# A GNN, mixer and FFN block on one core: the input norm written out with three buffers of x, and the first gathers and products placed inside the batch statistics

## The reference

```python
xn = _layernorm(x)
x = x + gnn(xn, edge_weight, W1, b1, W2, b2, eps, src, dst) + mix(xn[None])[0]
x = x + ffn(_layernorm(x)[None])[0]

def gnn(x, edge_val, ...):
    agg = jax.ops.segment_sum(edge_val[:, None] * x[edge_src], edge_dst, num_segments=N)
    h = jax.nn.relu(((1.0 + eps) * x + agg) @ W1.T + b1)
    return h @ W2.T + b2

def mix(x, ...):
    h = logmap0(proj(x, c), c)                    # a factor for each node
    h = conv1d(h, w_qkv, pad=2)                   # for a sequence of one: a 256 to 768 product
    h = relu(batchnorm(h, bn_gamma, bn_beta))     # mean and variance over all nodes
    ...                                           # linear attention in groups of 32, w_res, expmap0
```

## Time and profile before

| | us |
|---|---|
| median of 3 runs (2632.32 to 2636.76) | 2632.83 |
| the profiled execution: its time | 2637.63 |
| its span in the profile | 2636.0 |
| PE busy | 2489.5 (94%) |
| DVE busy | 1806.4 (69%) |
| ACT busy | 1464.7 (56%) |
| POOL busy (issuing gathers for the most part) | 1753.3 (67%) |

### The profile page before, as it was taken

One profiled execution on the slowest core, in us unless ns is written; L12 is line 12 of the kernel. 1 busy time (PEld: TensorE's weight loads), 2 busy tenths in 40 slices (PEclk: granted clock), 3 DMA queues, 4 the chain that ended last, 5 costly groups with the idle time before them and its releaser, 6 DMA issues.

```text
span 2636.0 us, 42907 instructions
## 1 busy us (share of the span) xinstructions
PE 2489.5 (94%) x12654; PEld 2172.5 (82%) x12654; DVE 1806.4 (69%) x5986; ACT 1464.7 (56%) x3513; POOL 1753.3 (67%) x1858
## 2 busy tenths in 40 slices
PE   5688899999999999999999999999999999999997
PEld 4466688888888888888888888888788888888886
DVE  5754676767767677776776867667676776777657
ACT  4453555655556565565655556556565655656531
POOL 0006777777777777777777777777777777777600
PEclk9798999999999999999999999999999999999998
DMA  7433444344444444434344444443434444343338
GB/s 228 153 115 88 119 118 127 114 121 124 120 125 115 120 124 120 125 116 128 115 121 123 117 126 114 121 123 115 126 115 126 118 121 121 111 129 114 108 116 278
DMA packets 195537, 333.37 MB, mean 126 GB/s; under 512 B 47839, under 2 KB 138013, under 8 KB 195209
## 3 DMA queue, kind: packets, MB, share of 16 engines
q0 software_dynamic: 85216, 233.60, 31.1%
q1 hardware_dynamic: 105018, 92.42, 10.9%
q10 hardware_dynamic: 5072, 4.57, 0.6%
HBM read 291.99 MB, written 38.46 MB: 125 GB/s over the span
## 4 chain that ended last, share of the span: by engine, by line
PE 76%; DVE 9%; ACT 6%; DMA 6%; issue 2%; ACTq 1%; POOL 1%; SPq 0%; DVEq 0%; POOLq 0%
PE bank L1168 23%; PE qkv L1263 13%; PE bank L1275 12%; PE bank L1182 9%; PE bank L1212 6%; PE qkv L1192 4%; DMA work<-in_x 4%; PE qkv L1191 2%; PE bank L1228 2%; PE bank L1237 2%; PE bank L1202 2%; DVE rings L975 2%; DMA rings<-xn_dram,window 1%; DVE work L407 1%; ACT work L465 1%
## 5 line engine op out<-in xcount | busy, mean ns | idle before, releaser
L781 POOL DMA_INDIRECT rings<-xn_dram,window x1764 | 1740.5, 987 | 651.3 <-issue 381.4
L1168 PE MATMUL bank<-rings 128*128 128x256 f32 x3528 | 891.9, 381 | 28.1 <-DMA rings<-xn_dram,window 16.3
L1168 PEld LDWEIGHTS bank<-rings 128*128 128x128 f32 x3528 | 654.6, 190 | 130.2 <-DVE rings L975 32.8
L975 DVE TENSOR_SCALAR rings<-iota,window_dst,window 128x128 f32<-128x128 f32 x1764 | 559.8, 364 | 150.3 <-PE bank L1168 136.2
L1263 PE MATMUL qkv<-work,ffn_weights 128*128 128x256 f32 x1568 | 362.9, 380 | 0.0
L1275 PE MATMUL bank<-ffn_weights,work 128*128 128x256 f32 x1568 | 362.0, 379 | 0.0
L871 ACT ACTIVATE work<-qkv,fb 128x256 f32<-128x256 f32 x392 | 159.6, 472 | 310.5 <-PE qkv L1263 309.9
L1275 PEld LDWEIGHTS bank<-ffn_weights,work 128*128 128x128 f32 x1568 | 297.2, 190 | 40.0
L1263 PEld LDWEIGHTS qkv<-work,ffn_weights 128*128 128x128 f32 x1568 | 293.9, 190 | 37.8
L1182 PE MATMUL bank<-resident,weights 128*128 128x256 f32 x1176 | 279.0, 381 | 0.0
L1182 PEld LDWEIGHTS bank<-resident,weights 128*128 128x128 f32 x1176 | 224.5, 191 | 30.7
(11 more groups left out here) (222 smaller groups left out, 3332.5 us busy)
## 6 DMA issues: line engine op xcount, KB each, us to landing
rings<-xn_dram,window POOLq DMA_INDIRECT x1764, 2.8
xn_dram<-work SPq DMA_DIRECT2D x14, 896.0 KB, 7.7
work<-xn_dram SPq DMA_DIRECT2D x49, 256.0 KB, 3.1
work<-in_x SPq DMA_DIRECT2D x48, 256.0 KB
out<-work SPq DMA_DIRECT2D x48, 256.0 KB
work<-in_x SPq DMA_DIRECT2D x13, 896.0 KB, 5.9
rings<-out SPq DMA_DIRECT2D x6, 896.0 KB, 8.6
out<-rings SPq DMA_DIRECT2D x6, 896.0 KB, 6.8
```

The costliest lines, as they stand in the source:

```text
L781: nc.gpsimd.indirect_dma_start(out=msg[q][:, :], out_offset=None, in_=xn_dram[:, :], in_offset=bass.IndirectOffsetOnAxis(ap=window[t % WIN ...
L975: v.tensor_scalar(sel[k % SEL_RING], iota[:, :], window_dst[b][:, k % SLOTS:k % SLOTS + 1], window[b][:, k % SLOTS, 2:3].bitcast(F32), ALU ...
L1168: te.matmul(agg[h][:, 0:D], sel[k % SEL_RING], msg[q], start=first, stop=last, skip_group_check=True).then_inc(slot_used, 1)
```

## The change

Names of files' lines below are those before (-) and after (+); the rest of the program is the same.

- **Norm.** `x` has three buffers (the third in the ring of `msg`). All 14 groups are written out. DVE's work is split: `stats(g)` and `result(g)`, in the order stats 0, stats 1, result 0, stats 2, result 1, stats 3, and so on. In `result` the logarithm's input is made before the normalised rows are written.
- **ACT** asks for the logarithm ahead of the copies of the group before, and then takes copy and scale by turns. It issues no loads: the 21 loads of the weights are POOL's (`params_pool`), behind the first transfers of the tables.
- **Tables.** `tables_ends` is DVE's first work, `tables_chunks` comes after result 2, `tables_borders` after result 4. The load of `dst` is POOL's first instruction.
- **Start of the main loop.** The dummy product that frees the ring comes before the batch statistics. DVE makes the first 12 one-hots, and PE does the means' products, two thirds of `mix_h1(0)` and the first 12 edge products, inside the statistics. The products of the Gram matrix go to other PSUM banks.

```diff
+        xb = [view(work, 0, G, D), view(work, 1792, G, D), view(rings, 11 * D, G, D)]
+            for g in range(3):
+                load(g)
+            for g in range(NG):
+                sp.wait_ge(xn_ready, g + 1)
+                if g + 3 < NG:
+                    load(g + 3)
+                store(g)
...
+            tables_ends(dve)
+            stats(0)
+            stats(1)
+            for g in range(NG):
+                result(g)
+                if g == NG - 4:
+                    dve.wait_ge(xn_ready, NG - 3)
+                    v.memset(xb[(NG - 1) % 3][:, G - 1], 0.0).then_inc(xlast_clear, 1)
+                if g == 2:
+                    tables_chunks(dve)
+                if g == 4:
+                    tables_borders(dve)
+                if g + 2 < NG:
+                    stats(g + 2)
...
+            rsqrt_table(0)
+            for g in range(NG):
+                if g + 1 < NG:
+                    rsqrt_table(g + 1)
+                log(g)
+                for k in range(G):
+                    if g > 0:
+                        copy(g - 1, k)
+                    scale(g, k)
...
+            early(0, 6)
             dve.wait_ge(gw_done, 1)
...
             ins.then_inc(gw_read, 1)
+            early(6, EARLY_EDGES)
             dve.wait_ge(stat_done, 1)
...
             pe.wait_ge(bounds_landed, 16)
+            pe.wait_ge(h0T_ready, NT)
+            te.matmul(agg[0][:, 0:1], ident[:, :], ident[:, 0:1], start=True, stop=True).then_inc(slot_used, RING)
+            bn_products(pe)
+            mix_h1(0, 0)
+            mix_h1(0, 1)
+            bn_moments(pe)
+            for k in range(EARLY_EDGES):
+                edge(0, k)
             pe.wait_ge(bn_ready, 1)
-            te.matmul(agg[0][:, 0:1], ident[:, :], ident[:, 0:1], start=True, stop=True).then_inc(slot_used, RING)
-            te.matmul(agg[0][:, 0:1], ident[:, :], ident[:, 0:1], start=True, stop=True).then_inc(rem_used, 1)
-            for q in range(3):
-                mix_h1(0, q)
+            te.matmul(agg[1][:, 0:1], ident[:, :], ident[:, 0:1], start=True, stop=True).then_inc(rem_used, 1)
+            mix_h1(0, 2)
```

More of the change, by code:

```diff
@@ L22 @@
 LEAD = 8
+EARLY_EDGES = 12
 WINDOWS = 4
@@ L353, in norm_sync @@
         def norm_sync(sp):
[L354 to L377, removed]
+            def load(g):
+                if g < NG - 1:
+                    sp.dma_start(xb[g % 3], node_rows(x, g * G, G)).then_inc(x_landed[g % 3], 16)
+                else:
+                    sp.dma_start(xb[g % 3][:, 0:G - 1], node_rows(x, g * G, G - 1)).then_inc(x_landed[g % 3], 16)
+                    sp.wait_ge(xlast_clear, 1)
+                    sp.dma_start(xb[g % 3][0:LAST, G - 1], x[(NT - 1) * P:N, :]).then_inc(x_landed[g % 3], 16)
@@ L379, in build, with store, norm_vector, stats @@
+            def store(g):
+                sp.dma_start(node_rows(xn_dram, g * G, G), xnb[g % 2]).then_inc(xn_stored[g % 2], 16)
+            for g in range(3):
[5 more added lines that the diff above has]
+                store(g)
         stats_ready = sem("stats_ready")
-        def norm_vector(dve, stats_turn):
+        def norm_vector(dve):
             v = nc.vector
-            def step(g, h, landed, before):
+            def stats(g):
+                h = g % 2
+                link = Link(dve, stats_link, 1, g)
+                part, mv, var = view(st[h], 0, G, 6), view(st[h], 42, G, 2), norm_cols(h)[0]
+                dve.wait_ge(x_landed[g % 3], 16 * (g // 3 + 1) + (16 if g == NG - 1 else 0))
+                for k in range(G):
+                    ins = v.bn_stats(part[:, k], xb[g % 3][:, k])
+                ins.then_inc(stats_ready, 1)
+                dve.wait_ge(stats_ready, g + 1)
+                for k in range(G - 1):
+                    v.bn_aggr(mv[:, k], part[:, k])
+                link(v.bn_aggr(mv[:, G - 1], part[:, G - 1]))
+                v.tensor_scalar(var[:, 0], mv[:, :, 1], LN_EPS, None, ALU.add)
+                v.tensor_scalar(var[:, 1], mv[:, :, 1], TINY, None, ALU.add).then_inc(var_ready, 1)
+                link.close()
+            def result(g):
+                h = g % 2
@@ L396, in step @@
[L396 to L400, removed]
                 dve.wait_ge(rsqrt_seed, g + 1)
                 newton(v, link, y, var, t)
-                if before is not None:
-                    dve.wait_ge(xn_stored[h], before * 16)
-                    dve.wait_ge(h0_ready, before * (2 * G) + (h - 1) * G)
@@ L1071, in step @@
                     nxt = ahead >= STEP_SLOTS
-                    if not (last and nxt):
+                    if not (last and nxt) and not (i == 0 and ahead < EARLY_EDGES):
                         edge(i + nxt, ahead % STEP_SLOTS)
@@ L1116, in step, with early @@
                     tail.close()
-            dve.wait_ge(bounds_landed, 16)
-            start_tile(0)
-            for k in range(LEAD):
-                edge(0, k)
+            def early(first, n):
+                if first == 0:
+                    dve.wait_ge(bounds_landed, 16)
+                    start_tile(0)
+                for k in range(first, n):
+                    edge(0, k)
+            bn_vector(dve, early)
             for i in range(NS):
```

163 lines of the change are left out of this document (61 added, 102 removed).

## The result

| | before, us | after, us |
|---|---|---|
| median of 4 runs each | 2633.18 (2632.32 to 2636.76) | 2601.06 (2598.36 to 2602.23) |
| the profiled execution: its time | 2637.63 | 2601.07 |
| its span | 2636.0 | 2599.4 |
| start of the Gram products (A) | 188.10 | 166.72 |
| start of step 2 (B) | 307.73 | 267.35 |

The changed kernel is faster: ratio 0.9874, 95% interval 0.9857 to 0.9891. By the medians that is 32.1 us, by the two profiled executions 36.6. The forecast was 49.8 for the profiled pair, and by medians a time of 2583: the measured 2601.06 is 18 above it. A came 21.4 earlier (32 forecast), B 40.4 (49.7 forecast), and behind B some of it went again.

What follows compares the result with a forecast made beforehand. Latency (DVE's waits) bounds the norm, then POOL's gathers set the pace to B. A = 156, B = 258 against 307.7: 49.8 off 2637.63 gives 2587.8, by medians 2583; forecast proper 2575 to 2591, range 2572 to 2604.

Steps and rivals of the forecast that it cites:

- the rivals at 2593 to 2596: Longer norm period 2596 (0.22), steps 0 and 1 bound by their chain 2593 (0.10), POOL's issues blocking DVE 2595 (0.06).
- a longer period of the norm: Norm: slow-landing loads or PE at low clock lengthen each group, to 8.8 us for a load; 2596, chance 0.22.
- Length of a group: Norm: DVE's 10.34 us per group without its three waits becomes 7.80; not below PE's 7.6.
- Loads moved to POOL: Norm: weights' loads run beside x from about 18 us, exposing only group 3's load; cost taken as 0, at most 4.
- The other tables: Norm: tables_chunks and tables_borders block DVE 17.8 us as before, including 4.21 waiting for the gather of borders.
- Start: Start of the norm: dst lands at 9.5 us (bounds 8 and 14), first factor ready at 26.3.
- Last group: End of the norm: last factor at 145.5, plus PE's tiles and low-clock restart, gives A = 156, 32 earlier.
- A to B: First mixer product at A + 31.2, new POOL wait 4.1, B at A + 101.9, so 258.
- B hangs on when the first gather goes, and not on the chain: Steps 0 and 1: 72 gathers at 1.30 us, 93.6 us, set the pace; B comes 97.6 after the first.
- the rival with the chain as the bound: Steps 0 and 1: without edges to fill with, PE waits for ACT and DVE in the mixer; 10 us lost, 2593, chance 0.10.
- An earlier start is kept: Behind B: PE and POOL are close, and the earlier start stays whichever bounds; 49.8 us off the profiled execution.
- The rival on POOL's issues and DVE: Norm: DVE waits while POOL writes descriptors; 21 issues of 0.55 give up to 11.6 us, 2595, chance 0.06.

Runs made afterwards that it cites:

- the experiment: Changed kernel with POOL issuing the 21 weight loads ahead of the tables' transfers: 2992.84 us against before's 3029.73, ratio 0.9887.
- The experiment that asks earlier: Changed kernel with the gather of borders asked for right after the chunks, used after result 4 as before: 2990.71 us, ratio 0.9874 to before.
- the first pair: The original measurement of the kernel before and the changed kernel, chip not on record: medians 2633.18 and 2601.06 us, ratio 0.9874.
- the four chips: Chips of the follow-up runs, where every kernel takes 15 to 16% longer than at first; the kernel before takes 3029.73 to 3052.34 us.
- second chip: Before 3050.42 us; changed kernel 3026.86; changed norm with the ring freed after the batch statistics and no early one-hots, mix_h1 or edges 3024.47.
- first chip: Before 3029.73 us; changed norm with ring freed after the statistics 3004.05; changed kernel with ring freed early, no early edge products 2999.57.
- without the early edges: Changed kernel with no edge product before step 0 and 8 early one-hots for 12, ring still freed early: 2999.57 us, ratio 0.99 to before.
- both waits gone: Changed kernel with weights' loads ahead of the tables' and borders asked for early: 3005.01 us, ratio 0.9853; repeated 3008.05, 0.9869.

## Why the prediction was right in direction, and 13 us too high in gain

The time of 2601.06 lies inside the forecast range of 2572 to 2604, near its far end, and outside the 2575 to 2591 of the forecast proper. What carried the range so far up were the rivals at 2593 to 2596, and the likeliest of them, a longer period of the norm, did not come about. So the range held in part by luck. One sign that the prediction had named for being wrong did appear, once: x's landing ended a wait of DVE. By the prediction's own steps:

- **Length of a group: right, and on the safe side.** 7.80 was taken, DVE takes 7.41. All three waits went as worked out. PE with 7.6 is therefore the bound, not DVE. Its restart "at the low clock", taken as 1, cost 1.6 behind the borders; from 120 to 140 the clock is 1.00.
- **Loads moved to POOL: the step that failed.** "Taken as 0, at most 4"; it is 8.29, and the experiment puts it down to the weights. The prediction counted the queues' time for x alone, at 77%, and set the weights beside it without adding their bytes. In the window from 20 to 40 the DMA engines are at 92%, and x takes 15.8 us to land. The 10 us of `tables_chunks`, which were to let the queues drain, come after the wait and not before it.
- **The other tables: mis-sized.** The 4.21 for the borders were carried over; it was 7.59. The wait before, as a window, and the wait after:

```profile
88.00:94.40 6.40, 0.00 (x0) 0.00 (x0) 2.13 (x4) 0.00 (x0) 2.04 (x2) 0.64 0.07 16
```

```profile
76.00:84.20 8.20, 8.20 (x47) 7.04 (x46) 0.63 (x4) 5.97 (x31) 2.05 (x2) 1.00 0.86 257
```

The gather had the DMA engines to itself (7% busy) and now runs beside x at 86%; a gather of borders takes 6.3 us from issue to landing, and took 2.5. The experiment that asks earlier gains 9.5 at A.
- **Start: mis-sized.** `dst` let DVE go at 11.71, not 9.5; it was inside the bounds of 8 to 14. First factor at 28.06, not 26.3.
- **Last group.** Start 1.8 late, x 8.3, borders 3.4, less 13 x 0.39 = 5.1 for the shorter group, make 8.4; the last factor was 7.5 late (153.03, 145.5 forecast). From there to A it took 13.7, not 10.5, because PE had a backlog as the new bound. Together 10.7: A at 166.72, not 156.
- **A to B: right in the sum (100.6, forecast 101.9), but by other terms, which is luck in part.** The means took 2.73 and the second moments 2.99, not 5.2 each, and with this the first mixer block stood at A + 24.2 and not A + 31.2. The 0.50 of the earlier trace rows did not come back, and the rows put this down to the new order behind A (no kernel here has that order with the old norm, which would show it alone). The kernel before had the full clock at A as well, and lost it behind a stand; a window of its Gram products, its first one-column products, and a window of the changed kernel's means:

```profile
188.10:193.50 5.40, 5.40 (x16) 2.95 (x16) 1.18 (x7) 0.00 (x0) 0.00 (x0) 1.00 0.01 2
```

```profile
195.57 1.02 PE L595 MATMUL bank<-rings,work 128*128 128x1 f32 x4 [2.04 <-DVE work L567]
```

```profile
172.00:174.60 2.60, 2.60 (x26) 2.60 (x24) 2.42 (x7) 0.00 (x0) 1.99 (x3) 1.00 0.40 112
```

  Before, PE stood 2.04 us for DVE between the two, and the clock was 0.50 from 196 on. Now the means and `mix_h1`, which need nothing from DVE, fill that place, and PE does not stand between A and 190. (It is at 0.90 in the second moments and at 0.79 in the twelve edges, 6.85 us for a forecast of 7.2.) The prediction had this order in its list and priced it at the old clock.

  Of the 7 us so gained 4.9 went again in step 0: from its first mixer block to step 1 it took 228.81 - 190.87 = 37.9, for a forecast of 33. There PE stood 7.32 for ACT, did the second mixer block at 0.50 in 3.8 us instead of 2, and stood 1.94 for a one-hot. Step 1 took 267.35 - 228.81 = 38.5, as forecast (38.3).

  POOL waited 0.69 and 1.21 where 0.30 is usual, 1.3 more and not 4.1. And "B hangs on when the first gather goes, and not on the chain" was true of the kernel before and is not of the changed one, in which PE waits for no gather up to B. This is the rival with the chain as the bound (0.10), hidden by the gain in the statistics.
- **"An earlier start is kept": not in full in this pair.** The gap was 40.4 at B, 43.1 at step 3, and 36.6 at the end. Single steps differ by up to three us either way between the two executions. The last step that lies between two starts, as a window of after and of before:

```profile
2421.80:2471.90 50.10, 45.88 (x220) 38.77 (x219) 29.30 (x93) 25.45 (x55) 24.48 (x55) 0.93 0.30 83
```

```profile
2461.80:2508.70 46.90, 42.94 (x220) 36.60 (x219) 29.19 (x93) 25.34 (x55) 26.45 (x56) 1.00 0.33 92
```

The same 220 products took 2.94 more of PE's time, at a granted clock of 0.93 instead of 1.00. That is 2.9 of the 6.5 us lost between step 3 and the end. Why the clock fell there in one and not in the other no run shows; the other 3.6 us are not explained.

**The rival on POOL's issues and DVE** did not come about. The changed kernel's POOL at two of the 21 issues, and its DVE at the same time, which writes normalised rows:

```profile
20.81 0.78 POOL L193 DMA_DIRECT2D weights<-in_wqkvT  x1
...
28.45 0.54 POOL L193 DMA_DIRECT2D cols<-in_br  x1
```

```profile
25.73 2.41 DVE L415 TENSOR_SCALAR work<-work 128x256 f32<-128x256 f32 x7
```

Seven rows of L415 took 2.41 beside the issues and 2.35 at 114.51 without. An issue took 0.54 to about 0.8, which is the 0.55 of the earlier trace rows and up to half as much again; in all they were done at 33.8, and nobody waited for them. By the Trainium skill (SBUF — State Buffer, "SBUF: two separate sides") one of the two waits for the other where the DVE instruction holds the port pair that they share. No such wait is in these rows; whether L415 holds the pair they do not show. The move to POOL did cost, but in the DMA engines and not at the port.

**What stays open.** That the early start is worth the 19 us at B (119.6 to 100.6) in the first pair is read from two profiles alone. The one-column products are in it, with 4.7 us less on PE's chain (2.73 and 2.99 where they took 10.4), which is their order and clock and not the early gathers. At the pace of the four chips it is worth between -2.4 us (3024.47 - 3026.86, second chip) and 4.5 (3004.05 - 2999.57, first chip, without the early edges), inside the intervals. No kernel that separates the two was measured at the pace of the first pair. There, the norm's 21.4 of the 36.6 are the part that the experiments bear out.

**The best version** of those run is the changed kernel with both waits gone, with or without its early edges: 0.9843 to 0.9869 of before, where the changed kernel has 0.9919, 22 to 27 us faster than it on the one chip where they ran beside each other.

## What to carry to other kernels

When a transfer is moved in time or to another queue, add its bytes to those of its new neighbours: here a share of 77% for one stream left no room for a second, and the first one paid in time to landing. When a loop is made to run without waits, its outer waits grow by what the loop now asks of the DMA engines, so a small dependent transfer in it should be asked for a group or two before it is needed. A stand of PE was paid twice here: behind stands of 2.04, 7.32 and 7.85 us it went on at a clock of 0.50 to 0.56. So put work that needs nothing into such a gap, as the means and `mix_h1` are here. And a move of work is only worth what the next bound lets through: here 4.9 of 7 us won on PE's chain were gone before the next step.

## What the hardware showed that was not expected

- **The same program at two paces.** Of the changed kernel's chain of waits, the shares by what they were spent on, first in the first pair and then on the second of the four chips:

```profile
PE 78%; DVE 9%; DMA 5%; ACT 5%; issue 1%; SPq 0%; POOL 0%; DVEq 0%; POOLq 0%
```

```profile
PE 54%; another core or an unknown queue 14%; ACT 14%; DVE 8%; issue 8%; DMA 2%; SPq 0%; POOL 0%; ACTq 0%; DVEq 0%; POOLq 0%
```

  2601 us in the one and 3027 in the other, with the norm equal to within 1 us (A 166.72 and 166.11). DVE's and POOL's busy times are the same, and 22% of the chain is time in which no engine's work is what is waited for. It is seen in the stretch that has gathers: on the short one-column products, and on ACT's first work behind a mixer block, which waits at this pace for no named releaser behind 45 of the 98 blocks, 275 us in all, and never in the first pair. What holds them up is not settled by these runs.
- **An issue that waits.** SP's issue of a store, about 0.6 us otherwise, took 5.31 at a time when loads of x took 15.8 us and stores 13.7 to land, and the issue of a load just ahead of it took 2.32 and not 0.37. Nothing was due behind it until 51.45, so here it delayed nothing.
- **One-column products** took 2.73 us for 12 products (24 records) at a clock of 1.00 in the changed kernel. In the kernel before DVE waited 10.49 for 24 products (twice as many records) with the clock at 0.50: twice as long for each.
